# Deformable convolution on one core: the sampled values go through a DRAM scratch to their new partitions, and the convolution moves to the last of six rounds

## What is computed

```python
x = x + _L0_conv_ref(_gn(x), ...)   # spectral terms and a 1x1 mix
x = x + _L1_conv_ref(_gn(x), L1_conv_w_om, L1_conv_b_om, L1_conv_weight, L1_conv_bias)
```

```python
om = lax.conv_general_dilated(x, w_om, ...) + b_om
vals = jax.vmap(_bilinear_sample)(x, ys, xs) * mask[:, None]
out = jnp.einsum('bckhw,ock->bohw', vals, weight.reshape(Oc, -1, K2)) + bias
```

## Time and profile before

| what | us |
|---|---|
| median of three runs | 2205.14 |
| lowest and highest run | 2180.73 and 2221.71 |
| span of the profiled execution | 2204.3 |
| PE busy in it | 1875.0 (85%) |
| DVE busy | 1707.6 (77%) |
| ACT busy | 1630.4 (74%) |
| POOL busy | 1377.4 (62%) |

### The profile page before, as it was taken

How to read it: one execution, slowest core, us unless ns; L and a number is a source line. 1 busy time by engine, 2 the same in 40 slices (tenths; PEclk the granted TensorE clock), 3 DMA queues, 4 the chain that set the end, 5 groups by cost and what they waited for, 6 DMA issues and landing times.

```text
span 2204.3 us, 126941 instructions
## 1 busy us (share of the span) xinstructions
PE 1875.0 (85%) x50241; PEld 1307.4 (59%) x50241; DVE 1707.6 (77%) x2942; ACT 1630.4 (74%) x2854; POOL 1377.4 (62%) x1803
## 2 busy tenths in 40 slices
PE   8566169988999888898999899999999999999995
PEld 3321046655666555565666666666666666666663
DVE  8689358866888667686888788888888888888883
ACT  0003358877888777787888888888888888888883
POOL 0000057766777666676777777777777777777772
PEclk9699679999999999999999999999999999999997
DMA  9026636655666555655666666666666666666663
GB/s 339 1 114 252 255 104 173 172 142 140 175 172 172 144 143 152 160 151 145 173 172 173 160 169 177 172 172 172 172 172 172 172 175 169 170 171 173 172 165 92
DMA packets 196603, 364.84 MB, mean 166 GB/s; under 512 B 39760, under 2 KB 122480, under 8 KB 192368
## 3 DMA queue, kind: packets, MB, share of 16 engines
q1 hardware_dynamic: 196464, 362.74, 58.7%
HBM read 159.38 MB, written 52.22 MB: 96 GB/s over the span
## 4 chain that ended last, share of the span: by engine, by line
PE 45%; DVE 16%; issue 13%; POOL 4%; SPq 3%; ACT 2%; DVEq 2%; DMA 1%; POOLq 0%; ACTq 0%
PE pV L987 14%; PE pE L966 10%; DVE big L753 9%; PE pM L1012 8%; PE pM L999 7%; PE pR L1026 3%; SPq L421 3%; DVE halves L748 3%; DVE big L734 3%; POOL halves L493 2%; POOL prod L484 2%; PE pM L1033 1%; ACT halves L588 1%; DVE big L761 1%; DMA v<-big 1%
## 5 line engine op out<-in xcount | busy, mean ns | idle before, releaser
L753 DVE COPY big<-pE 128x768 f32<-128x768 f32 x768 | 725.7, 945 | 256.4 <-PE pE L966 246.3
L493 POOL TENSOR_TENSOR halves<-prod,halves 128x300 f16<-128x300 f32 x768 | 604.4, 787 | 429.8 <-DVE halves L748 275.8
L594 ACT ACTIVATE big<-pE 128x768 f32<-128x768 f32 x768 | 634.5, 826 | 112.3 <-PE pE L966 111.5
L987 PE MATMUL pV<-big 128*32 128x144 f32 x16384 | 671.7, 293 | 26.5 <-issue 22.6
L484 POOL TENSOR_TENSOR prod<-big 128x300 f32<-128x300 f32 x768 | 558.7, 728 | 73.3
L966 PE MATMUL pE<-big,sel_s 32*128 32x64 f16 (+1 forms) x24576 | 412.8, 203 | 144.6 <-DVE big L753 98.9
L966 PEld LDWEIGHTS pE<-big,sel_s 32*128 32x128 f16 x24576 | 324.8, 92 | 346.8 <-issue 300.6
L987 PEld LDWEIGHTS pV<-big 128*32 128x32 f32 x16384 | 440.2, 110 | 78.1 <-issue 33.7
L734 DVE STREAM_TRANSPOSE big<-halves 128x384 f32<-128x384 f32 x768 | 439.1, 572 | 28.8 <-POOL halves L493 7.2
L608 ACT ACTIVATE big<-pV 128x432 f32<-128x432 f32 (+1 forms) x640 | 304.8, 476 | 65.2 <-PE pV L987 36.0
L1026 PE MATMUL pR<-ident,strips 128*128 128x128 f32 x2048 | 335.8, 287 | 4.4 <-issue 4.4
(11 more groups left out here) (73 smaller groups left out, 1250.4 us busy)
## 6 DMA issues: line engine op xcount, KB each, us to landing
v<-big SPq DMA_DIRECT2D x1536, 96.0 KB
win<-xh_scratch SPq DMA_DIRECT2D x128, 544.0 KB, 3.9
big<-xh_scratch SPq DMA_DIRECT2D x384, 136.0 KB, 2.6
xh_scratch<-win SPq DMA_DIRECT2D x32, 544.0 KB, 2.7
big<-in_x SPq DMA_DIRECT2D x16, 1024.0 KB, 16.7
x_scratch<-big SPq DMA_DIRECT2D x16, 1024.0 KB, 3.9
x1r<-x_scratch SPq DMA_DIRECT2D x128, 128.0 KB, 2.1
out<-outs SPq DMA_DIRECT2D x128, 128.0 KB, 1.8
```

Of the source, the lines that this page charges most:

```text
L493: nc.gpsimd.tensor_tensor(half[:, rn % 2, :, 0:SQ, 1], prod[:, rn % 2, :, :], half[:, rn % 2, :, 0:SQ, 0], ALU.subtract).then_inc(low_done, 1)
L594: nc.scalar.activation(*expanded(1 - q, r, 0), ACT.Copy).then_inc(e_act, 1)
L753: nc.vector.tensor_copy(*expanded(1 - q, r, 1)).then_inc(e_dve, 1)
L987: last = mm(pV[r % 2][b * C:(b + 1) * C, o:o + TAPC], XT[q][:, t * P + b * C:t * P + (b + 1) * C], av[:, b * NT + t, :], start=True, stop= ...
```

## The change

The samples of a pair go out of `VS[q]` to a new DRAM tensor `vs_scratch` in one transfer of 128 partitions x 9216 bytes, in the place in SP's order where the twelve moves stood. In the next step, after the loads of rows and window and ahead of the output store, SP waits for that store to land and loads the three tap rows into `v2`, 32 channels x 4 images x 3072 bytes each. The evacuations of pV into `VS[q]` now wait for the store (`vs_st`) in place of the moves (`v2_ld`). CONV_AT goes from 4 to 5, on PE and DVE. The regions are still turned for each pair.

```diff
-OM_AT, OMT_AT, SIG_AT, ABS_AT, RELU_AT, CONV_AT = 0, 1, 2, 3, 4, 4
+OM_AT, OMT_AT, SIG_AT, ABS_AT, RELU_AT, CONV_AT = 0, 1, 2, 3, 4, 5
-NV2 = IPG * KS
+NV2 = KS
+        vs_d = nc.dram_tensor("vs_scratch", (2 * P, KS * KS * PX), fp32, kind="Internal").ap()
+            def load_samples(n, q):
+                wait(sp, conv_done, n)
+                sp.nop(nofuse=True)
+                sp.wait_ge(vs_st, (n + 1) * 16)
+                sp.nop(nofuse=True)
+                for ky in range(KS):
+                    taps = vs_d[q * P:(q + 1) * P, ky * KS * PX:(ky + 1) * KS * PX]
+                    sp.dma_start(v2[ky * C:(ky + 1) * C, :, :, :].rearrange("c b k n -> c b (k n)"),
+                                 taps.rearrange("(b c) n -> c b n", b=IPG)).then_inc(v2_ld, 16)
...
                 if on[-1]:
                     load_strips(N + 1, 1 - q, place)
+                if on[3]:
+                    load_samples(N - 3, 1 - q)
                 if on[3]:
                     g, local = place(N - 3)
                     sp.wait_ge(out_ready, N - 2)
...
                 if on[2]:
                     sp.wait_ge(v_act, (N - 1) * VN[1])
                     sp.wait_ge(v_dve, (N - 1) * VN[0])
-                    wait(sp, conv_done, N - 2)
-                    for b in range(IPG):
-                        for ky in range(KS):
-                            sp.dma_start(v2[ky * C:(ky + 1) * C, b, :, :].rearrange("c k n -> c (k n)"),
-                                         VS[q][b * C:(b + 1) * C, ky * KS * PX:(ky + 1) * KS * PX]) \
-                                .then_inc(v2_ld, 16)
+                    sp.nop(nofuse=True)
+                    sp.dma_start(vs_d[q * P:(q + 1) * P, :], VS[q]).then_inc(vs_st, 16)
...
-                            wait(act, v2_ld, (N - 3) * (16 * NV2))
+                            wait(act, vs_st, (N - 3) * 16)
...
-                            wait(dve, v2_ld, (N - 3) * (16 * NV2))
+                            wait(dve, vs_st, (N - 3) * 16)
```

More of the change, by code:

```diff
@@ L230, in build @@
         wino_ld = [sem(f"wino_ld{i}") for i in range(2)]
+        vs_st = sem("vs_st")
         v2_ld = sem("v2_ld")
```

## The result

| | before | after |
|---|---|---|
| median, us | 2204.70 | 2773.06 |
| lowest to highest run, us | 2180.73 to 2221.71 | 2742.93 to 2803.41 |
| span of the profiled execution, us | 2204.3 | 2801.6 |
| PE busy | 1875.0 (85%) | 2136.1 (76%) |
| moved by DMA, MB | 364.84 | 515.91 |

The changed kernel is slower by a quarter: ratio 1.254, 95% interval 1.242 to 1.267. The prediction had 1.4% and a range that ended at 2410 us.

A forecast was written before the change was run, and what follows sets the result against it. PE's program order was taken to bound the kernel, at 14.08 us a pair with the moves hidden. 2204.3 + 126 x 0.22 (28) gives 2232, plus 3 us for occasional transfer waits: 2235 us, 1.4% more, range 2135 to 2410.

The forecast's parts named there:

- What bounds the kernel, and the gap: PE's order sets the 14.08 us period; its 0.75 us gap only moves from round 0 to round 5.
- 126 x 0.22: 126 overlapped pairs, each 0.22 us longer (14.08 to 14.30) as round 0's sampling waits for L614: 28 us.
- The loop: Store, loads, convolution, L780, output issue, store: closes in 14.17 us against the engines' 14.30, cover 0.2 us.
- transfers late: Rival: PE's convolution waits for `v2`, from a chain of 10.7 us upward; 2405 us, at the bound 2520; chance 0.22.
- The price of the chain: From issue of the samples' store until the convolution can start: 10.5 us taken, bounds 9.1 and 12.9.
- More stalls: Rival: the heavier queue lengthens PE waits that have no releaser, twice 30.7 us plus slow clock; about 2270 us; chance 0.05.
- The range: Whole-kernel time of 2135 to 2410 us, leaving out the best faster and worst late-transfer cases.

The follow-up runs named there:

- The kernel with the loop open: Changed kernel with samples loaded ahead of rows and window, and the samples' store issued ahead of the output store; 2232.4 us, ratio 1.015.
- B: Transfers-only kernel, nothing else running: the changed kernel's three sample loads, each into one block of 32 partitions; 7.47 us.
- C: Transfers-only kernel: three loads of the same bytes with the same 3072-byte packets, into all 128 partitions; 5.27 us.
- the transfers by themselves: A separate kernel doing nothing but transfers, each group waited for before the next; store 4.22 us, the twelve moves of before 9.15 us.
- D: Transfers-only kernel: the three sample loads, each into every third of 96 partitions instead of a block of 32; 6.98 us.
- the fastest kernel: Kernel before with DVE's addition L780 put off to round 5 and the twelve moves issued ahead of the output store; 2083.8 us, ratio 0.960.

## Why the prediction was wrong

**What bounds the kernel, and the gap.** Right. The convolution in round 5 gives 14.30 us as worked out, with both new waits in their places (0.68 for 0.86 us ahead of `expand`, 0.30 for 0.23 ahead of the sampling). The term 126 x 0.22 stands. Its measured ratio, 1.040 with an interval from 1.022, is more than that term's 1.3%. Uneven steps add 86 us to the profile of that run against 70 in before; the rest of the difference isn't explained.

**The loop.** Right as a mechanism, and it was the rival "transfers late": store, loads, convolution, L791 (L780 before), output issue, store. The kernel with the loop open is at 14.30 us and 2232 us; the forecast was in effect the time of that kernel. The rival had 0.22, and even its upper end, 2520 us, was too low.

**The price of the chain.** This is the step that failed: "I take 10.5", with 12.9 as its upper bound. Measured are 13.90 us, outside the bounds. The store was 5.14 us instead of 4.3; it was 4.57 where the rows' loads weren't queued behind it. The loads took 8.76 instead of the 6.3 that were left for them (10.5 + 0.1 - 4.3). Alone they take 7.47, where the prediction's own price of a transfer, 1.18 MB at 366 GB/s plus 1.04 us, gives 4.3. Of these 3.2 us the destination of 32 partitions is 2.2 (B against C in the transfers by themselves), and 1.0 lies in the part that isn't data: even one load of 1.18 MB into all partitions takes 5.22 us. So the whole is 4.22 and 7.47 us alone, 0.85 more inside the kernel, and 1.36 for rows and window: 13.90. The DMA engines were nearly always busy, as the prediction had assumed, but at 253 GB/s in place of 366. I had priced the loads at the rate of loads into 128 partitions, and said that large packets made that the nearest row. The nearer row was the line that the change removes: moves into 32 partitions each. And the upper bound was taken from a stretch of mixed traffic, where the narrow loads are a small part.

The Trainium skill (SBUF — State Buffer, Door 1: The DMA port swizzle) states that a transfer's bandwidth depends on how many of the 16 SBUF ports its partitions reach, and that 32 adjacent partitions reach 8 of them, half. The trace agrees for the narrow loads: 197 GB/s with all DMA engines full. By the Trainium skill's limit of about 218 GB/s for 8 ports the loads take, as an estimate, 1.18 MB / 218 GB/s = 5.4 us of data. It is the rule that spoke against the loads as they are written, and the prediction didn't have it. That the ports are the cause isn't shown: loads spread over partitions 0 to 95 gained only 0.5 us alone (D).

The rule of the Trainium skill (DMA: Bandwidth & Descriptors, Latency and other measured facts) that the prediction weighed and set aside, of some 2 us of fixed cost, is nearer than 1.04 for a load: one takes 5.22 us, of which 3.2 are data at 366 GB/s and 2.0 aren't. For the store it isn't: 4.22 us leave 1.0, although its target is DRAM, where that rule has the cost heaviest.

**The clock.** Missing in the sum. The part of the loop from the convolution's start to the next store was put at 3.57 us and measured 4.94, since the convolution runs at 1.2 GHz after PE's wait of over 2 us; at full clock, with the same chain, it was 3.62. In all 14.17 + 3.30 (the chain, 13.90 against 10.5 and 0.1 for the semaphores) + 1.37 (the clock) gives the 18.84 us of the step. Against 14.08 and over 126 pairs that is 600 us (587 by the median period of 18.74); the profiled execution has 597 more than before.

**More stalls.** Not the cause: eight steps of the changed kernel take over 4 us more than the median, 68 us in sum, against seven and 61 us before.

**The range.** It ended at 2410, inside the rival's case. The transfers decide from a chain of 10.7 us upward, and the prediction's bounds were 9.1 and 12.9 us, so more than half of this interval costs one for one; a flat reading of these bounds would have made the slower case the likelier one.

## What to carry to other kernels

A transfer that is hidden has a slack; before it is replaced, work out the whole loop through which its end releases its next start, and test the new path against that loop. A round trip through DRAM is two landings in a row, and what is queued ahead of it on the issuing engine adds to it (rows and window cost 1.4 us here): two changes of order in one queue were worth 540 us here, with not a byte less moved. Part of such a price is the clock that the waiting engine loses, 1.1 us a step here. Look for the partitions that a transfer writes, not only for its bytes and packets, and when one engine's gap is closed by moving an instruction, look at which engine's next wait was under its cover.

## What the runs showed of the hardware

Three loads of 384 KB into 32 adjacent partitions each take 7.47 us and into 128 partitions 5.27, with the same packets. Every third partition of 96 gives 6.98 alone, and yet 5 to 7% in the kernel.

PE's granted clock fell from 1.00 to 0.50 within a wait of 2.5 us, in a step in which PE was otherwise busy but for a gap of 0.7 us; waits of 0.7 us, in every step, left it at 1.00. With six matmuls more ahead of the wait, which leave 0.2 to 0.6 us of it in most steps, it stayed at 1.00.

PE's code is fetched in some steps while the loop runs. Seven in the profile of before take 8 to 10 us more than the others; in each of the seven, five packets pass on the instruction queue, and in 89 of the 122 steps from 400 us on none does. Sixteen matmuls more, which are 32 instructions in a step of some 390, raise the packets from 117 to 561, six longer ones, 12 instructions, to 307, and with these the stalls end at about 1950 us. The size of the code isn't all: the fastest kernel has PE's code of before unchanged, and has 53 packets and no such step. Where the limit lies isn't shown. Here a few instructions more in the loop body cost far more than the instructions take.
